# Transposing edge counts by a DMA instead of by TensorE in a two-layer graph kernel

## What is computed

```python
h = relu(layernorm(x))
# layer 0: relational convolution
hn = ln_weight * h * rsqrt(mean(h*h) + 1e-6)
z = hn @ W_root + bias
for r in (0, 1):
    w = (edge_type == r)
    z += segment_sum(hn[src] @ W_rel[r] * w, dst) / max(segment_sum(w, dst), 1)
x1 = x + h + elu(z) @ wo
# layer 1: graph attention
g = relu(layernorm(x1)); p = g @ W; al, ar = p @ a_l, p @ a_r
e = exp(-leaky_relu(al[src] + ar[dst], 0.1))
out = x1 + elu(segment_sum(e * p[dst], src) / (segment_sum(e, src) + 1e-5))
```

## Time and profile before

| | us |
|---|---|
| median of 3 runs | 532.58 (531.64 to 536.67) |
| profiled execution, its own time | 530.4 |
| its span | 528.6 |
| busy: TensorE / VectorE / ScalarE / GpSimd | 502.6 / 368.9 / 231.3 / 74.6 |
| counting stage, 118.8 to 258.6 | 139.8 |
| one step of it from step 3 on | 12.7 |

### The profile page before, as it was taken

How to read it: one execution, slowest core, us unless ns; L and a number is a source line. 1 busy time by engine, 2 the same in 40 slices (tenths; PEclk the granted TensorE clock), 3 DMA queues, 4 the chain that set the end, 5 groups by cost and what they waited for, 6 DMA issues and landing times.

```text
span 528.6 us, 7977 instructions
## 1 busy us (share of the span) xinstructions
PE 502.6 (95%) x3073; PEld 433.2 (82%) x3073; DVE 368.9 (70%) x634; ACT 231.3 (44%) x386; POOL 74.6 (14%) x72
## 2 busy tenths in 40 slices
PE   3989999997899999998999999999999999999995
PEld 2889989997789999998778888888787888888885
DVE  4836885578798888855875555554798887777633
ACT  5855443407856666668733332221333322222112
POOL 1362213100000000000000000000073322222400
PEclk9999999999899999999999999999999999999998
DMA  9862273304013233225951111100022222222211
GB/s 259 223 224 79 78 236 104 118 1 110 1 50 107 81 120 115 79 79 167 311 191 39 40 39 40 39 1 0 1 78 79 78 78 79 78 79 78 79 41 41
DMA packets 22186, 49.15 MB, mean 93 GB/s; under 512 B 4798, under 2 KB 10709, under 8 KB 22018
## 3 DMA queue, kind: packets, MB, share of 16 engines
q1 hardware_dynamic: 21887, 48.33, 30.5%
q0 software_dynamic: 256, 0.26, 0.2%
HBM read 33.05 MB, written 16.85 MB: 94 GB/s over the span
## 4 chain that ended last, share of the span: by engine, by line
PE 84%; DVE 8%; ACT 5%; issue 1%; DMA 1%; SPq 0%; DVEq 0%; ACTq 0%
PE ps L1208 13%; PE ps L1433 9%; PE ps L1340 9%; PE ps L1434 9%; PE ps L1435 9%; PE ps L1414 6%; PE ps L1416 6%; PE ps L1415 6%; PE ps L1301 3%; PE ps L1363 2%; PE ps L1385 2%; PE ps L1397 1%; PE ps L1387 1%; PE ps L1386 1%; PE ps L1234 1%
## 5 line engine op out<-in xcount | busy, mean ns | idle before, releaser
L1433 PE MATMUL ps<-h_hi,att_hi 125*125 125x512 f32 (+1 forms) x190 | 73.5, 387 | 0.0
L1434 PE MATMUL ps<-h_lo,att_hi 125*125 125x512 f32 (+1 forms) x190 | 72.6, 382 | 0.0
L1435 PE MATMUL ps<-h_hi,att_lo 125*125 125x512 f32 (+1 forms) x190 | 72.5, 382 | 0.0
L1414 PE MATMUL ps<-wg,gT_hi 128*125 128x512 f32 x160 | 64.0, 400 | 0.5 <-DVE wg L1014 0.4
L1416 PE MATMUL ps<-wg,gT_lo 128*125 128x512 f32 x160 | 63.1, 394 | 0.0
L1415 PE MATMUL ps<-wg,gT_hi 128*125 128x512 f32 x160 | 63.0, 394 | 0.0
L1340 PE MATMUL ps<-msg_hi,adj_hi 125*125 125x288 f32 x200 | 56.9, 308 | 0.6 <-ACT adj_hi L579 0.5
L1340 PE MATMUL ps<-msg_lo,adj_hi 125*125 125x286 f32 x200 | 51.7, 297 | 0.0
L1208 PE MATMUL ps<-w_hi,hT_hi 128*125 128x430 f32 x128 | 46.5, 363 | 0.1
L1208 PE MATMUL ps<-w_hi,hT_lo 128*125 128x430 f32 x128 | 45.9, 358 | 0.0
L1208 PE MATMUL ps<-w_lo,hT_hi 128*125 128x430 f32 x128 | 45.7, 357 | 0.0
(11 more groups left out here) (203 smaller groups left out, 1058.8 us busy)
## 6 DMA issues: line engine op xcount, KB each, us to landing
xt<-in_x SPq DMA_DIRECT2D x10, 448.0 KB
xh_scratch<-xt SPq DMA_DIRECT2D x10, 448.0 KB
xt<-xh_scratch SPq DMA_DIRECT2D x10, 448.0 KB
x_scratch<-xt SPq DMA_DIRECT2D x10, 448.0 KB
x1t<-x_scratch SPq DMA_DIRECT2D x10, 448.0 KB
xr<-x_scratch SPq DMA_DIRECT2D x10, 448.0 KB
out_x<-xr SPq DMA_DIRECT2D x19, 224.0 KB
wg_raw<-in_L_gnn_W SPq DMA_DIRECT2D x8, 512.0 KB, 9.1
```

What stands on the lines that cost most here:

```text
L1414: M.matmul(to, hi, wg[k][:, 0, cut], start=n == 0, stop=False)
L1433: M.matmul(to, hi[:, s, :], h_hi[:, s, cut], start=s == 0, stop=False)
L1434: M.matmul(to, hi[:, s, :], h_lo[:, s, cut], start=False, stop=False)
L1435: return M.matmul(to, lo[:, s, :], h_hi[:, s, cut], start=False, stop=s == TILES - 1)
```

## The change

In the branch that is executed, TensorE no longer transposes counts and ScalarE no longer copies them out. VectorE gets a function `summed`, which adds the two types of a tile's 16-bit counts into one buffer `sum_16`, and ScalarE gets `counts_turned`, which issues a transposing DMA from `sum_16` into `counts` on its own queue. `adj_16` becomes an unsigned 16-bit tensor, `counts` gets rows of 128 for each pair of tiles. `y_transposed` waits for `yT_lo_rdy` where it waited for the copied counts. The last two weight loads of layer 1 wait for all transfers where they waited for the last transposes. In the tails `transposed2(0, 0, 0)` stands later.

```diff
+        counts = sb(ctx, "counts", [P, TILES, TILES, SRCS], U16)
...
-                    sp.wait_ge(S["c_ps"], 3 * data(TILES - 1))
+                    sp.wait_ge(S["ct_out"], 16 * TILES)
...
+            def counts_turned(t, b, d):
+                act.wait_ge(S["sum_16"], data(t))
+                act.dma_start(counts[:, t], sum_16[:].rearrange("p n s -> p (n s)"), transpose=True).then_inc(S["ct_out"], 16)
...
-                pipeline((counted(0), 0), (y_split, 2), (counted(1), 0), (counts_part(0), 1), (counted(2), 0), (elu, 1), (counts_part(1), 1),
-                         (counted(3), 0), (counts_part(2), 1), (counted(4), 0), opening=split_wo, before=2, steps=(0, TILES))
+                pipeline((counted(0), 0), (y_split, 2), (counted(1), 0), (counted(2), 0), (counts_turned, 2), (elu, 1),
+                         (counted(3), 0), (counted(4), 0), opening=split_wo, before=2, steps=(0, TILES))
+                counts_turned(TILES - 2, 0, 4)
...
+            def summed(t, b, d):
+                mine = slice(T * b, T * (b + 1))
+                dve.wait_ge(S["win_16"], done(nth(t, NG - 1)))
+                if t == 0:
+                    V.memset(sum_16[:], 0).then_inc(S["pad_rdy"], 1)
+                    dve.wait_ge(S["pad_rdy"], 1)
+                else:
+                    dve.wait_ge(S["ct_out"], 16 * t)
+                V.tensor_tensor(sum_16[0:T, :, 0:T], adj_16[:, 0:TILES, mine], adj_16[:, TILES:BLOCKS, mine], ALU.add).then_inc(S["sum_16"], 1)
...
-                pipeline((one_hots(0), 0), (one_hots(1), 0), (y_split, 3), (one_hots(2), 0), (z_of, 2), (one_hots(3), 0), (y_of, 2),
+                pipeline((one_hots(0), 0), (summed, 2), (one_hots(1), 0), (y_split, 3), (one_hots(2), 0), (z_of, 2), (one_hots(3), 0), (y_of, 2),
                          (one_hots(4), 0), (lambda t, b, d: split_wo() if t == 0 else None, 2), (output1, 3), steps=(0, TILES))
+                summed(TILES - 2, 0, 4)
                 y_split(TILES - 3, 1, 3)
...
-                transposed2(0, 0, 0)
+                summed(*last)
                 z_of(*last)
                 y_of(*last)
+                transposed2(0, 0, 0)
                 output1(*before)
...
-                pipeline((counted(0), 0), (y_transposed, 2), (summed(0), 1), (counted(1), 0), (summed(1), 1), (counts_part(0), 1), (counted(2), 0),
-                         (output1(0), 2), (counts_part(1), 1), (counted(3), 0), (output1(1), 2), (counts_part(2), 1), (counted(4), 0), steps=(0, TILES))
+                turned = lambda t, b, d: y_transposed(t, b, d, True)
+                pipeline((counted(0), 0), (turned, 2), (summed(0), 1), (counted(1), 0), (summed(1), 1), (counted(2), 0),
+                         (output1(0), 2), (counted(3), 0), (output1(1), 2), (counted(4), 0), steps=(0, TILES))
```

More of the change, by code:

```diff
@@ L576, in counts_evicted @@
                     act.wait_ge(S["s_ps"], room(t))
-                    act.wait_ge(S["c_ps"], 3 * room(t))
+                    if usual:
+                        act.wait_ge(S["sum_16"], room(t))
+                    else:
+                        act.wait_ge(S["c_ps"], 3 * room(t))
                 bank_of = counts_bank(NG * b + g)
@@ L704, in _ @@
                 norm2(0, 0)
-                counts_part(0)(*last)
                 norm2(1, 1)
+                counts_turned(*last)
+                back_to_exp()
+                elu(*last)
                 transposed2(0, 0, 0)
[L708 to L711, removed]
                 y_split(*last)
@@ L1099, in counted_in @@
                 dve.wait_ge(S["att_e"], data(t))
[L1100 removed]
+                V.scalar_tensor_tensor(att[b][:], att[b][:], FINITE, counts[0:T, :, t, 0:T], ALU.min, ALU.mult).then_inc(S["att_p"], 1)
             def low_part(t, b):
@@ L1343, in summed, with counts_transposed @@
                 return relation
-            def counts_transposed(more, parts=range(3)):
-                def tile(t, b, d):
+            def counts_transposed(t, b, d):
                     mine = slice(T * b, T * (b + 1))
-                    for c in parts:
+                    for c in range(3):
                         if c == 0:
-                            pe.wait_ge(S["win_out" if more else "win_16"], done(nth(t, NG - 1)))
+                            pe.wait_ge(S["win_out"], done(nth(t, NG - 1)))
                         if c != 1:
@@ L1358, in tile, with y_transposed @@
                             for r in range(RELS):
-                                if more and r == RELS - 1 and s == some[-1]:
+                                if r == RELS - 1 and s == some[-1]:
                                     rest_too(done(nth(t, NG - 1)), *[(to[v], adj_lo[:, q * TILES + v, mine], ident_r[0:T, 0:CB])
                                                                     for v in some for q in range(RELS)])
-                                part, unit = (adj_hi, ident_r[0:T, 0:CB]) if more else (adj_16, ident_16[0:T, 0:CB])
-                                last = M.matmul(to[s], part[:, r * TILES + s, mine], unit, start=(s == some[0] and r == 0),
+                                last = M.matmul(to[s], adj_hi[:, r * TILES + s, mine], ident_r[0:T, 0:CB], start=(s == some[0] and r == 0),
                                                 stop=(r == RELS - 1), skip_group_check=True)
                         last.then_inc(S["c_ps"], 1)
-                return tile
-            def y_transposed(t, b, d):
+            def y_transposed(t, b, d, usual=False):
                 pe.wait_ge(S["y_rdy"], data(t))
-                pe.wait_ge(S["c_used"], 3 * t + 2 + 3 * CREDIT)
+                if usual:
+                    pe.wait_ge(S["yT_lo_rdy"], room1(t))
+                else:
+                    pe.wait_ge(S["c_used"], 3 * t + 2 + 3 * CREDIT)
                 for n in range(2):
@@ L1488, in _ @@
                     for b in range(2):
-                        for stage in (summed(0, True), summed(1, True), counts_transposed(True), y_transposed, output1(0), output1(1)):
+                        for stage in (summed(0, True), summed(1, True), counts_transposed, y_transposed, output1(0), output1(1)):
                             stage(d * 2 + b, b, d)
```

38 lines of the change are left out of this document (17 added, 21 removed).

## The result

| | before | after |
|---|---|---|
| median of 4 runs each, us | 533.24 (531.64 to 536.67) | 611.77 (610.04 to 613.62) |
| profiled execution, its own time / span, us | 530.4 / 528.6 | 613.38 / 611.6 |
| one ordinary step of the counting stage, us | 12.7 | 20.6 |

The ratio is 1.1503, with a 95% interval of 1.1461 to 1.1546: the change costs 15%, as forecast (609, range 572 to 665). The steps cost less than forecast and the tail more.

What follows compares the result with a forecast made beforehand. TensorE, busy 95%, was taken as the bound. Eight stalls of 9.6 us plus 1.7 of clock add 90.4, less 11.7 of identity matmuls: +78.7 on 530.4 gives 609.1 us, range 572 to 665.

Steps and rivals of the forecast that it cites:

- The circle: Counting steps 2 to 9: VectorE's addition awaits ScalarE's late transfer, and TensorE's output1 awaits VectorE; 8 stalls.
- The length of a pause: TensorE ahead of output1(0): casts, transfer, addition, one-hots, split and last link sum to 9.6 us, ends 7.0 and 13.7.
- L: Time from issue to landing of the counts transfer: 5.0 us taken, ends 2.4 and 9.1.
- Both casts: ScalarE's two casts of the third group, ahead of the transfer's issue in each stall: 1.49 us.
- The clock: TensorE behind each stall: half of 3.5 us at the 1.2 GHz level lost, 1.7 us charged, ends 0 and twice that.
- What went: Identity matmuls removed from TensorE's chain: about 1.17 us a step, 11.7 us for ten tiles.
- The tail: End of the counting stage and layer 1's weight loads: reordering and last transfer together counted as 0 us.
- Those about cancel: In the tail, 0.94 and 0.46 us of waits saved against later transposed2, residual (1.22 us) and last y_split: 0.
- The wait doesn't bite: Rival at VectorE's addition: the transfer lands before the next addition, steps bound by VectorE's 11.6 us, 521 us; chance 0.03.
- Ten blocks one after another: Rival for the transfer: its ten 128×128 blocks go serially, 642 us or more; chance of landing time over 9 us 0.17.
- A short transfer: Rival for the transfer: landing in 2.4 us gives 588 us; chance of ending under 588 us 0.16.
- a clock that holds: Rival on TensorE's clock: no loss behind stalls, with a 2.4 us landing besides, 575 us; within the 0.16 for under 588.

Runs made afterwards that it cites:

- copy_lag1: Changed kernel with a plain copy for the transposing transfer, issued one step earlier in ScalarE's order, against that plain-copy kernel: 527.55 us, 0.9915 of the kernel before.
- copy_two_buffers: Changed kernel with a plain, equally late transfer, plus two alternating sum buffers, against the one-buffer plain-copy kernel: 529.14 us, 0.9942 of the kernel before.
- copy_twice: Changed kernel with a plain transfer, each done twice, the second issued after the first landed, against the plain-copy kernel (599.66 us): 641.75 us.
- copy_warm: Changed kernel with a plain transfer, plus 27 unread matmuls on TensorE ahead of its wait in output1(0), against the plain-copy kernel (599.66 us): 593.35 us.
- copy_lag1_tail: As copy_lag1, with the end-of-stage order put back to that of the kernel before: 525.01 us, 0.987 of the kernel before.

## Why the prediction was right, and where its terms were off

**The circle.** Right, and now shown, with a plain transfer whose pauses sum to the same 57.6 us: VectorE waits for a transfer that ScalarE issues only behind TensorE's third group, and TensorE's next product waits for VectorE. `copy_lag1` and `copy_two_buffers` each break one link and lose all of it; `copy_twice` lengthens one and pays eight times. The count of 8 was right too.

**The length of a pause.** Forecast 9.6, measured 7.1. Two terms of the sum were too large. *L*: 5.0 taken, 3.35 to 3.66 measured in seven of the ten transfers. The row nearest to it was the store of 500 KB with 3.1 us; I had leaned on rows with another kind of transfer. The ends, 2.4 and 9.1, held but for the last landing; the lower one was read 0.7 too low, since L runs from the issue, from which that store needs 3.1, and 2.4 is counted from the end of its issue. *Both casts*, 1.49: the transfer is issued beside the second, so 0.6. The addition (0.82 taken, 0.819 measured), the one-hots, the split and the last link were right. A step came to 20.6 for 22.8, by these two.

The Trainium skill (VectorE: DVE Perf Modes, "The three transpose paths") led to an estimate of 13.1 us for the ten blocks; the trace doesn't agree: ten blocks in one transfer land in 3.4. The estimate of 3.7 from the Trainium skill (DMA: Bandwidth & Descriptors, "Latency and other measured facts") is close.

**The clock.** The 3.5 us at 0.50 were right, and the loss is a little more than the 1.7 charged. Behind the pause that ends at 195.83, by the chain of waits:

```profile
195.83 0.79 PE ps L1404
...
199.18 0.73 PE ps L1320 x10
```

The seven matmuls of the product take 3.35 us for 1.70, the ten of the group behind them 0.73 for 0.46, in all 1.9. Given back it is worth 1.5 to 1.6, by `copy_warm`.

**What went.** 11.7 us, and with it the parts come out: 9.8 of it stood ahead of the last step's product, 1.9 behind. Up to the first product there are 7.3 of pause, 1.3 of the late first cast and 2.2 of the low clock behind it, less 1.6 of identity matmuls and the 0.7 that TensorE had waited there before: 8.5 for the 8.4 measured, though the chain there isn't the same in both kernels. In the seven steps there are 50.3 of pauses and 7 × 1.9 of clock, less 8.2: 55.4 of the 56.4 measured. The late first cast and the clock behind it I had not priced. About 1 us stays unassigned.

**The tail.** Counted at 0, measured 18.1. This is the step that failed, in both of its sentences. "Those about cancel": the new order costs about 3.5, by `copy_lag1_tail`. "Lands with L of 5 at 252.3 [...]: 0": I used one L for all transfers, and put the last one into a stretch in which weights and tiles are moved. It landed after 18.8. With the plain copy, in the same place, 8.5; the same tail is then 296.8. That the transposing one suffers more in a crowd is so in one trace; its cause stays open, since it wasn't run alone.

The total is close, 609 for the profiled 613.4, because two errors cancelled, and that is luck: 78.7 forecast for all that comes up to the last step's product and 64.9 measured, 13.8 too many, and 18.1 of the tail left out.

**The rivals.** *The wait doesn't bite* named the right point of decision, the transfer half a step earlier or a second buffer. Its 521 us was 7 too low by `copy_lag1` (527.55, with a plain transfer): it left out the late start and the tail. *Ten blocks one after another* and *a clock that holds* are out, by the landing and by the clock's rows. *A short transfer* at 2.4 us was nearer to the truth than my forecast for L, and still gave less than the total, for want of the tail.

## What to carry to other kernels

Where one engine waits for a transfer that another issues, write down for both what stands in front of the issue and what stands behind the wait: a pause is their whole sum, and it comes back with every step, however short the transfer. Issue the transfer in the step in which its data are ready or give it a second buffer; moving a single consumer ahead of the wait gave 8 of 72 us here, since a third engine still stood behind it. And ask for the landing of a transfer in the stretch in which it goes out, not for its median.

## What the hardware showed beyond what I had expected

- A transfer on ScalarE's queue is issued while ScalarE's cast ahead of it still runs (both at 210.01). The issue alone took 1.36 us transposing and 0.60 plain. The last transposing one took 2.91, with a DMA share of 0.93 beside it, and ScalarE's next instruction stood 3.98 us.
- A transposing transfer of 320 KB inside SBUF landed in 3.4 us in quiet steps, some 0.2 more than a plain one of as many rows.
- The same transposing transfer took from 3.4 to 18.8 us. For the plain one, 3.2 to 10.3, it is shown that the traffic beside it does it.
- The granted clock fell to 0.50 at the start of the counting stage although TensorE had not paused there for long: in the changed kernel it ran groups of ten matmuls, some 0.6 us each, with waits of 1.25, 0.52, 0.51 and 0.49 us ahead of them.
